# Modulations by streaming matmuls, made layer by layer between the first groups; loads reordered; the next layer's first scores in the last MLP step

## The chip, the cores and the metric

One core of a Trainium2 chip runs the whole program in one launch. The metric is the device time in microseconds, lower is better. [...] An engine that waits holds back everything behind the wait in its stream.

## The reference

Four transformer layers on x of [32, 128, 144] (32 sequences, 128 tokens, 144 channels), each conditioned by a row of `cond` [32, 144]:

```python
mod = silu(c) @ w_ada + b_ada                  # [32, 864]
sh1, sc1, g1, sh2, sc2, g2 = split(mod, 6)     # tanh on the gates in layer 2
x = x + g1 * attention(norm(x) * (1 + sc1) + sh1)        # 16 heads of 9 channels
x = x + g2 * mlp(norm(x) * (1 + sc2) + sh2)              # hidden 576
```

Layer 0's MLP is a mixture of four experts with the best two weighted by softmax. Layers 0, 1 and 3 use LayerNorm; layer 2 uses RMS norm, and norms q and k by head too. All in float32; the weights come in float32.

## The kernel before

The 32 sequences are eight groups of four; a group has 512 tokens. x stays in SBUF (`X`). Because 144 = 128 + 16 channels, every product over channels is two matmuls: one over the first 128 and one over the 16 others, held in split form with the bias rows (66 rows, in float32r). `split_chunk` on VectorE makes that form of the weights, from a staging tile (3 slots) that `load_chunk` on SyncE fills.

**The head.** SyncE first issues the loads of `si`, `sir` (the condition, 128 and 16 rows), `ident`, `masks`, the block mask and four gains (L294 to L301, one semaphore `q_c`), then layer 0's modulation weights, X of the first 8 sequences (576 KB), the q/k/v and projection weights, the other three layers' modulation weights and the rest of X in one DMA (L315). Then it waits for each layer's gates and stores them to a scratch (L316 to L319), issues three more chunks and `far_weights()` (23 DMAs: q/k/v and projection weights of layers 1 to 3, the expert weights of layer 0), and only then enters `attention(0)`. ScalarE makes silu after all of `q_c`. TensorE then makes the modulations of all four layers (`layer_mods`, L480): the weights are the stationary operand and the condition, 32 columns, the moving one, for shift and scale of the main 128 channels; the same for the 16 others repeated four times (that copy is made by VectorE's `replicate`); and the gates the other way round, with 144 columns. VectorE moves the results into `modm` and `modr` (`take_mods`), ScalarE the gates into `gsb`. The engines enter `attention(0)` when all four layers are done.

**Attention.** A group goes through statistics (`stats`, VectorE), the factor (`factor`, GpSimd), normalisation (`rows` on GpSimd or `normalise` on VectorE), the copy of the 16 channels (`copies`), transposes (`t_main`, `t_rem`), modulation (`mod_main` ScalarE, `mod_rem` VectorE), rounding (`round_rem`, `split_rem`), and the q/k matmuls (`q_and_k`). q and k are split in three bf16 parts (`part1` ScalarE, `rest1` VectorE, `parts23` GpSimd), written to a DRAM scratch (`write_parts`, 4 DMAs) and read back in another layout (`read_parts`, 12 DMAs) into one of three slots of `qk`. Groups are prepared two ahead: q and k of group n+2 are made while group n is attended to.

A group's attention is eight units U of two times four heads. For each, `scores_for_max` (TensorE, banks 0 and 1) and `head_max` (VectorE) give the maxima of the rows, `turn_max` and `max_out` turn them, `scores` makes the scores again, transposed and with the maxima taken off, ScalarE's exp follows, then `weigh`, `to_tokens`, `normed`. `scores_for_max` runs AHEAD = 5 units before `scores`. At the start of a layer `start_layer` (L645) makes these five units first, each waiting for the maxima of the one before, as both use banks 0 and 1.

In the first half of the program the slots of `qk` also hold the modulation weights, so that the first reads of `read_parts` wait for the end of the modulations. After each group SyncE issues the load of the gates for the next (`load_gates`), and in layer 0 two chunks. In layer 1 it issues the MLP weights of layers 1 to 3 in one go after the first group (`late_weights`, L340, 18 DMAs).

**The MLP.** For each group: five hidden tiles (`first`, two matmuls each), gelu on ScalarE, then `second` for each of the four sequences (five accumulating matmuls, each two passes); four experts one after another in layer 0. On VectorE follow the weighting (`experts`) and the gated product (`gated`), and GpSimd adds to X. Other work of the next layer's first groups is woven in by `after_tile` and `after_seq`.

Of the kernel before, what the change touches and what calls it, by code (L numbers as in the profile page):

```python
# [7 lines left out]
F32 = mybir.dt.float32  # L8
# [9 lines left out]
HID = 576  # L18
E = 4
# [68 lines left out]
BY_POOL = [k for l in range(L) for k in ([0, 1, 2, 3] if l == 0 else []) + [turned_at(l, g) for g in range(1, 7)]  # L88
           + [16 * l + 10, 16 * l + 11]]
BY_DVE = [k for l in range(L) for g in range(8) for k in prepared_mlp(l, g)]  # L90
# [11 lines left out]
def build(nc, io):  # L102
    ctx = ExitStack()
    with ctx:
# [77 lines left out]
        maskf = prob_f[0:TB, 0:2 * T].rearrange("p (a t) -> p a t", a=2)  # L182
# [4 lines left out]
        def turned_v(n):  # L187
# [5 lines left out]
        gsb = parts[0:B].rearrange("p m a t -> p (m a t)").bitcast(F32)[:, 0:L * 2 * C].rearrange("b (l n) -> b l n", l=L)  # L193
        qk_f = qk[:].rearrange("p a r h t -> p (a r h t)").bitcast(F32)
        ada = qk_f[:, 0:L * 6 * C].rearrange("p (l n) -> p l n", l=L)
        adar = qk_f[0:CR_CH + 1, L * 6 * C:2 * L * 6 * C].rearrange("p (l n) -> p l n", l=L)
        ada4 = qk_f[:, 2 * L * 6 * C:2 * L * 6 * C + 2 * 2 * 4 * 4 * CR_CH] \
            .rearrange("p (a k n) -> p a k n", a=4, k=4)
# [11 lines left out]
        q_c, q_x0, q_x1, q_w0 = sem("q_c"), sem("q_x0"), sem("q_x1"), sem("q_w0")  # L210
# [4 lines left out]
        q_gs, q_out = sem("q_gs"), sem("q_out")  # L215
# [18 lines left out]
        g_x, g_ew, g_ox, d_xn = sem("g_x"), sem("g_ew"), sem("g_ox"), sem("d_xn")  # L234

# [44 lines left out]
        def _(sp):  # L280
            def load_chunk(i):
# [6 lines left out]
                sp.dma_start(stage[0:4 * CR_CH, staged(i), 0:n], src.unsqueeze(0).to_broadcast([4, CR_CH, n])) \  # L288
                    .then_inc(done, 16)
                if bias is not None:  # L290
                    sp.dma_start(stage[4 * CR_CH:REM, staged(i), 0:n], bias.unsqueeze(0).to_broadcast([2, n])) \
                        .then_inc(done, 16)

            sp.dma_start(si[:], io.cT[0:CM]).then_inc(q_c, 16)  # L294
            sp.wait_ge(d_set, CR + 1)
            sp.dma_start(sir[0:CR_CH], io.cT[CM:C]).then_inc(q_c, 16)
            sp.dma_start(ident[:], io.ident).then_inc(q_c, 16)
            sp.dma_start(masks[:], io.masks).then_inc(q_c, 16)
            sp.dma_start(maskf, io.block_mask).then_inc(q_c, 16)
            for i, a in enumerate(io.gains):  # L300
                sp.dma_start(gains[:, i:i + 1], a.unsqueeze(0).to_broadcast([128, 1])).then_inc(q_c, 16)  # L301
            sp.dma_start(ada[:, 0, :], io.ada_w[0][0:CM, :]).then_inc(q_ada[0], 16)
            sp.dma_start(adar[0:CR_CH, 0, :], io.ada_w[0][CM:C, :]).then_inc(q_ada[0], 16)
            sp.dma_start(adar[CR_CH:CR_CH + 1, 0, :], io.ada_b[0].unsqueeze(0)).then_inc(q_ada[0], 16)
            xv = io.x.rearrange("b t c -> t b c")
            sp.dma_start(X[:, 0:2 * G, :], xv[:, 0:2 * G, :]).then_inc(q_x0, 16)
            sp.dma_start(wqkv[:, 0, :], io.qkv_w[0][0:CM, :]).then_inc(q_w0, 16)
            sp.dma_start(wproj[:, 0, :], io.proj_w[0][0:CM, :]).then_inc(q_w0, 16)
            for i in range(NEAR):
                load_chunk(i)  # L310
            for l in range(1, L):
# [3 lines left out]
            sp.dma_start(X[:, 2 * G:B, :], xv[:, 2 * G:B, :]).then_inc(q_x1, 16)  # L315
            for l in range(L):  # L316
                sp.wait_ge(a_gt, CR + l + 1)
                sp.dma_start(gate_scr[l].rearrange("w b c -> b w c"), gsb[:, l, :].rearrange("b (w c) -> b w c", w=2)) \
                    .then_inc(q_gs, 16)  # L319
            for i in range(NEAR, NST + NEAR):  # L320
                load_chunk(i)
# [10 lines left out]
            def far_weights():  # L332
                for l in range(1, L):
                    sp.dma_start(wqkv[:, l, :], io.qkv_w[l][0:CM, :]).then_inc(q_w1, 16)
                    sp.dma_start(wproj[:, l, :], io.proj_w[l][0:CM, :]).then_inc(q_w1, 16)
                sp.dma_start(wgate[:], io.gate_w[0:CM, :]).then_inc(q_w1, 16)
                for e in range(E):
                    load_mlp(L - 1 + e, q_w1)

            def late_weights():  # L340
                sp.wait_ge(s_y, CR + y_base[1])
                for i in range(EARLY, len(chunks)):
                    load_chunk(i)
                for l in range(1, L):
                    load_mlp(l - 1, q_w2)
# [31 lines left out]
            def read_parts(l, n):  # L377
                p, r = n % 2, n % 3
                if n < 3:
                    sp.wait_ge(d_mod, CR + L)  # L380
                    sp.wait_ge(s_ada, CR + L)
                else:
# [41 lines left out]
            def attention(l):  # L424
                n0, m0 = 8 * l, 16 * l
                if l == 0:
                    sp.wait_ge(q_gs, 16 * L)
                    load_gates(0)
                    for n in range(2):
                        write_parts(0, n)  # L430
# [1376 lines left out]
```

## Time and profile before

| | us |
|---|---|
| median of 3 runs | 1697.54 (1695.68 to 1697.6) |
| the profiled execution | 1692.07 |
| its span | 1690.3 |
| TensorE busy | 1512.2 (89%) |
| VectorE busy | 957.0 (57%) |
| ScalarE busy | 817.0 (48%) |
| GpSimd busy | 544.2 (32%) |
| TensorE's part of the chain that ended last | 62% |
| DMA's part of it | 14% |

Shares are of the span. The chain is followed back from the last instruction, at each step to what released it. Times in the rows below are from the span's start. A row such as `[7.51 <-POOL xr L1635]` says that the engine stood idle for 7.51 us before the instruction, until GpSimd's write of `xr` at line 1635 released it. The rows of `SPq` are SyncE's issuing of DMAs, not the transfers.

### The profile page before, as it was taken

To read this page: it belongs to the slowest core of one execution; us is meant where nothing else is said; L and a number is where in the kernel's file an instruction comes from. 1 tells how busy PE (TensorE), PEld (TensorE's weight loads), DVE (VectorE), ACT (ScalarE), POOL (GpSimd) and SP (SyncE) were. 2 spreads that over 40 slices of the span, in tenths; PEclk is the share of its full clock that TensorE was granted. 3 is DMA by queue.
4 is the path that set the end of the run, shared out by engine and by line. 5 is a ranking of instruction groups with operands and counts; after the bars stand their busy time and mean duration, and the time that the engine had idled before them with its cause. 6 is when DMAs were issued, how large, how long until landed. Compare 5 with 4: busy or idle time off the path is not lost.

```text
span 1690.3 us, 42551 instructions
## 1 busy us (share of the span) xinstructions
PE 1512.2 (89%) x16240; PEld 1116.7 (66%) x16240; DVE 957.0 (57%) x2662; ACT 817.0 (48%) x1687; POOL 544.2 (32%) x751
## 2 busy tenths in 40 slices
PE   6659998999999998879899968878799899998998
PEld 4436666777777776656667746656577666766777
DVE  2368886233343333768744778898535566665442
ACT  0246676233333322657655436666554455555543
POOL 0535553111131210444432323424334324432321
PEclk9979999999999998989999979999899989998999
DMA  4445551000021020554501243443223767676021
GB/s 118 137 117 133 133 129 37 8 7 8 8 50 29 29 50 1 120 137 115 112 17 35 56 93 79 103 104 86 65 48 39 110 108 112 100 121 113 16 60 47
DMA packets 209275, 126.30 MB, mean 75 GB/s; under 512 B 143873, under 2 KB 192608, under 8 KB 203890
## 3 DMA queue, kind: packets, MB, share of 16 engines
q1 hardware_dynamic: 190386, 121.21, 32.8%
q10 hardware_dynamic: 18688, 2.36, 1.1%
q8 instruction: 132, 2.16, 0.6%
q14 instruction: 69, 0.57, 0.1%
HBM read 89.56 MB, written 33.18 MB: 73 GB/s over the span
## 4 chain that ended last, share of the span: by engine, by line
PE 62%; DMA 14%; DVE 9%; SPq 8%; issue 5%; POOL 1%; ACT 1%; DVEq 0%; POOLq 0%; ACTq 0%
PE bank L850 15%; PE bank L832 13%; DMA qk<-qk_scr 7%; PE bank L613 4%; PE bank L578 4%; PE bank L833 4%; DVE negm L1329 4%; SPq L403 3%; PE bank L641 3%; SPq L374 2%; PE bank L621 2%; PE bank L597 2%; PE bank L534 2%; DMA v_scr<-wfc 2%; PE bank L601 2%
## 5 line engine op out<-in xcount | busy, mean ns | idle before, releaser
L1061 ACT ACTIVATE prob<-bank 128x512 f32<-128x512 f32 x512 | 278.0, 595 | 245.9 <-PE bank L601 245.1
L1329 DVE TENSOR_REDUCE negm<-bank 128x4 bf16<-128x512 f32 x512 | 334.0, 682 | 104.2 <-PE bank L578 100.2
L1180 ACT ACTIVATE hid<-bank 128x512 f32<-128x512 f32 x280 | 166.7, 596 | 351.9 <-PE bank L833 351.2
L850 PEld LDWEIGHTS bank<-wfc,hid 128*128 128x128 f32 (+1 forms) x2240 | 285.8, 192 | 11.6 <-issue 9.1
L850 PE MATMUL bank<-wfc,hid 128*128 128x144 f32 (+1 forms) x2240 | 290.8, 287 | 0.2 <-DVE gx L1359 0.2
L832 PE MATMUL bank<-hT,wfc 128*128 128x512 f32 x560 | 290.4, 599 | 0.0
L1655 POOL TENSOR_TENSOR X<-X,gx 128x288 f32<-128x288 f32 x128 | 100.7, 800 | 429.7 <-DVE gx L1359 427.0
L833 PE MATMUL bank<-hr,rfc 66*128 66x512 f32 x280 | 224.7, 802 | 0.0
L578 PE MATMUL bank<-qk 54*128 54x128 bf16 (+1 forms) x2048 | 125.1, 245 | 94.0 <-DVE negm L1329 49.9
L613 PE MATMUL bank<-prob,V 128*32 128x128 f32 x4096 | 173.8, 290 | 2.4 <-ACT OT L1067 2.4
L597 PE MATMUL bank<-qk 54*128 54x128 bf16 (+1 forms) x2048 | 172.0, 239 | 4.1 <-ACT prob L1061 4.1
L601 PE MATMUL bank<-mT,pick 64*128 64x128 bf16 x2048 | 169.0, 229 | 0.0
L578 PEld LDWEIGHTS bank<-qk 54*128 54x128 bf16 (+1 forms) x2048 | 71.2, 103 | 141.0 <-DVE negm L1329 67.6
L1640 POOL CAST parts<-res 96x512 bf16<-96x512 f32 x96 | 59.2, 617 | 267.1 <-DVE res L1279 266.0
L1478 DVE SCALAR_TENSOR_TENSOR On<-bank,cw,On 128x144 f32<-128x144 f32 x96 | 30.8, 363 | 199.1 <-PE bank L850 199.1
L832 PEld LDWEIGHTS bank<-hT,wfc 128*128 128x128 f32 x560 | 102.0, 191 | 60.2 <-ACT hid L1180 33.2
L1266 DVE TENSOR_SCALAR hmod<-bank,modr 64x128 f32<-64x128 f32 x256 | 86.9, 396 | 90.7 <-PE bank L511 90.4
L613 PEld LDWEIGHTS bank<-prob,V 128*32 128x32 f32 x4096 | 100.9, 113 | 42.7 <-issue 27.0
L1008 ACT ACTIVATE hT<-bank,modm 128x128 f32<-128x128 f32 x256 | 98.5, 452 | 42.1 <-PE bank L504 42.1
L597 PEld LDWEIGHTS bank<-qk 54*128 54x128 bf16 (+1 forms) x2048 | 109.6, 102 | 9.2 <-ACT prob L1061 6.4
L1642 POOL TENSOR_TENSOR parts<-res,parts 96x512 bf16<-96x512 f32 x96 | 111.3, 1160 | 7.8
L1067 ACT ACTIVATE OT<-bank 128x256 f32<-128x256 f32 x256 | 99.2, 388 | 23.3 <-PE bank L613 11.4
(151 smaller groups left out, 2326.8 us busy)
## 6 DMA issues: line engine op xcount, KB each, us to landing
qk<-qk_scr SPq DMA_DIRECT2D x336, 72.0 KB
gbuf<-gate_scr SPq DMA_DIRECT2D x64, 288.0 KB, 4.0
qk_scr<-parts SPq DMA_DIRECT2D x48, 288.0 KB, 2.5
qk<-qk_scr SPq DMA_DIRECT2D x48, 216.0 KB
qk<-tok_scr SPq DMA_DIRECT2D x112, 72.0 KB
qk_scr<-parts SPq DMA_DIRECT2D x48, 144.0 KB, 2.4
qk<-qk_scr SPq DMA_DIRECT2D x48, 144.0 KB
tok_scr<-parts SPq DMA_DIRECT2D x48, 96.0 KB, 4.7
```

Source lines behind the costliest of these rows:

```text
L578: mm = pe.matmul(bank[s][:, T * i:T * i + T], operand(l, 0, n, U, s, i), operand(l, 1, n, U, s, i), start=True, stop=True)
L597: pe.matmul(bank[2 + s][:, at], operand(l, 1, n, U, s, i), operand(l, 0, n, U, s, i), start=True, stop=False)
L601: mm = pe.matmul(bank[2 + s][:, at], pick[half, 4 * (u % 2) + i, :], mT[half, u // 2, :], start=False, stop=True)
L613: mm = pe.matmul(bank[4][32 * i:32 * i + 32, T * s:T * s + T], V[:, n % 3, u // 2, VS * h:VS * h + 32], prob[:, 2 * (U % 2) + s, T * i:T * ...
L832: pe.matmul(bank[2 + i % 2][:], wfc1_t[:, at:at + 128], hT[:, h, :], start=True, stop=False)
L833: pe.matmul(bank[2 + i % 2][:], rfc1_t[:, at:at + 128], hr[:, h, :], start=False, stop=True) \
L850: mm = pe.matmul(bank[4 + q][:, C * (b % 2):C * (b % 2) + C], hid[0:rows, t, T * b:T * b + T], wfc2[0:rows, k, t, :], start=(t == 0), stop ...
L1061: act.activation(prob[:, 2 * (U % 2) + s, :], bank[2 + s][:], ACT.Exp, scale=scale).then_inc(a_exp, 1)
L1180: act.activation(hid[0:rows, t, :], bank[2 + i % 2][0:rows, :], func).then_inc(a_gelu, 1)
L1329: dve.tensor_reduce(negm[:, b, s, 4 * (u % 2):4 * (u % 2) + 4], bank[s][:].rearrange("q (h k) -> q h k", k=T), AX.X, ALU.max, negate=True) ...
L1642: pool.tensor_tensor(parts[:, m, 2, :], res[:, i % 2, :], parts[:, m, 1, :], ALU.subtract).then_inc(g_p3, 1)
L1655: pool.tensor_tensor(x, x, gx[:, q, :, :], ALU.add).then_inc(g_x, 1)
```

## The change

The modulations of a layer are now four matmuls: the condition is stationary (32 columns) and the weights stream, 432 columns for each half of a layer. Attention's and the MLP's half go to partitions 0 to 31 and 32 to 63 of bank 7. VectorE copies shift and scale out (`mods_out`), TensorE transposes them back to channels on partitions (`turn_mods`, four transposes into bank 4), VectorE adds the one and stores (`take_mods`), ScalarE takes the gates (`gates`). The four layers are placed between the steps of the first three groups. The modulation weights lie in other slots of `qk`, so that group 0's reads need not wait for them.

```diff
+            def layer_mods(l):
+                pe.wait_ge(q_ada[l], 48)
+                if l:
+                    pe.wait_ge(d_ms, CR + l)
+                    pe.wait_ge(a_gt, CR + l)
+                for w in range(2):
+                    out, cols = bank[7][B * w:B * w + B, 0:3 * C], slice(3 * C * w, 3 * C * w + 3 * C)
+                    pe.matmul(out, si[:], ada[:, l, cols], start=True, stop=False)
+                    mm = pe.matmul(out, sir[:], adar[:, l, cols], start=False, stop=True)
                 mm.then_inc(s_ada, 1)
+            def turn_mods(l):
+                pe.wait_ge(d_ms, CR + l + 1)
+                if l:
+                    pe.wait_ge(d_mod, CR + l)
+                for s in range(2):
+                    pe.transpose(bank[4][:, 2 * B * s:2 * B * s + 2 * B], mods_m[:, s, :], ident[0:2 * B, 0:2 * B])
...
```

TensorE's order in `attention(0)`, before `start_layer`:

```diff
+                    layer_mods(0)
+                    turn_mods(0)
                     t_rem(0, 5)
                     t_main(0, 6)
+                    for m in range(3):
+                        q_and_k(l, 0, m, m)
+                    layer_mods(1)
                     t_rem(1, 5)
                     t_main(1, 6)
                     values(l, 0, 0, 3)
                     values(l, 0, 1, 4)
                     for m in range(3):
+                        pe.wait_ge(d_r1, CR + m + 1)
                         q_and_k(l, 1, m, m)
+                    turn_mods(1)
+                    layer_mods(2)
                     t_rem(2, 5)
                     t_main(2, 6)
+                    turn_mods(2)
+                    layer_mods(3)
+                    turn_mods(3)
+                    pe.wait_ge(d_mod, CR + 4)
                     values(l, 1, 0, 3)
                     values(l, 1, 1, 4)
...
+                    pe.wait_ge(a_gt, CR + L)
+                    pe.wait_ge(d_set, CR + 3)
```

ScalarE has `gates(l)` at 0 before `mod_main(0)`, 1 before `mod_main(1)`, 2 before `mod_main(2)`, 3 after `round_rem(2)`. VectorE, which now normalises groups 0 to 2 in GpSimd's place:

```diff
+                    dve.wait_ge(q_x[0], 16)
                     stats(0)
+                    mods_out(0)
+                    split_chunk(0)
+                    normalise(0)
+                    take_mods(0)
                     stats(1)
                     mod_rem(0, 5)
                     split_rem(0)
+                    normalise(1)
                     for m in range(3):
                         rest1(0, m, m)
+                    mods_out(1)
                     mod_rem(1, 5)
                     split_rem(1)
+                    stats(2)
+                    normalise(2)
                     for m in range(3):
                         rest1(1, m, m)
+                    take_mods(1)
+                    mods_out(2)
                     mod_rem(2, 5)
                     split_rem(2)
+                    take_mods(2)
+                    mods_out(3)
+                    set_up()
+                    take_mods(3)
+                    split_chunk(1)
+                    dve.wait_ge(q_x3, 16)
                     stats(3)
```

(`head_max` of the first units follows; `set_up` holds the copies and memsets that stood before everything.) SyncE starts with the modulation weights; the small loads, the silu and the second chunk go to ScalarE's queue:

```diff
+            load_ada(0)
+            sp.dma_start(X[:, 0:G, :], xv[:, 0:G, :]).then_inc(q_x[0], 16)
+            load_chunk(0)
+            sp.dma_start(wqkv[:, 0, :], io.qkv_w[0][0:CM, :]).then_inc(q_w0, 16)
+            sp.dma_start(X[:, G:2 * G, :], xv[:, G:2 * G, :]).then_inc(q_x[1], 16)
+            load_ada(1)
+            sp.dma_start(X[:, 2 * G:3 * G, :], xv[:, 2 * G:3 * G, :]).then_inc(q_x[2], 16)
+            load_ada(2)
+            load_ada(3)
...
+                    write_parts(0, 0)
+                    read_parts(0, 0)
+                    for i in range(L):
+                        save_gates(i)
+                    write_parts(0, 1)
+                    read_parts(0, 1)
+                    sp.wait_ge(q_gs[0], 16)
                     load_gates(0)
+                    sp.dma_start(X[:, 3 * G:B, :], xv[:, 3 * G:B, :]).then_inc(q_x3, 16)
+                    for i in range(NEAR, NST + NEAR):
+                        load_chunk(i)
...
                     load_gates(m0 + g + 1)
+                    if l == 0 and g < 5:
+                        far_weights(g)
                     if l == 0 and 1 <= g <= 4:
                         for i in range(3 + 2 * g, 5 + 2 * g):
                             load_chunk(i)
-                    if l == 1 and g == 0:
-                        late_weights()
+                    if l == 1:
+                        late_weights(g)
```

`save_gates(l)` waits for the gates of layer l and stores them. `read_parts(0, 1)` waits for all modulations. `far_weights(g)` issues one expert's four DMAs and, for g of 1 to 3, two of layer g's weights; `late_weights(g)` the six chunk DMAs at g = 0 and four DMAs of one layer's MLP at g = 1, 3 and 5.

The first five units of layers 1 and 3 move into the last MLP step of the layer before (in layer 0 into the last expert's `second`):

```diff
+                    if l in (0, 2) and g == 7:
+                        if b == 0 and l == 0:
+                            pe.wait_ge(d_top, CR + 2 * 8)
+                        if b == 0 and l == 2:
+                            pe.wait_ge(q_mask, 16 * 12)
+                        scores_for_max(l + 1, UNITS * N + b)
+                        if b == 3:
+                            scores_for_max(l + 1, UNITS * N + 4)
...
+                            if g == 7 and e == E - 1:
+                                first_maxima()
                             for q in range(2):
                                 experts(g, e, q)
                         dve.wait_ge(d_y, CR + Y_OF[0] * (g + 1))
+                    if l == 2 and g == 7:
+                        first_maxima()
                     for q in range(2):
```

`first_maxima` is the ten `head_max` of those units. `start_layer` keeps the scores only for layers 0 and 2, with the turns of the maxima where they were.

## Rows read from the trace of the kernel before

**Rows 1.** Busy time by stretches: engines, granted clock, DMA share, GB/s.
```profile
13.60:52.70 39.10, 39.09 (x160) 27.95 (x160) 5.16 (x28) 1.20 (x3) 0.00 (x0) 1.00 0.34 94
...
10.00:27.50 17.50, 13.89 (x55) 10.69 (x56) 6.08 (x26) 0.75 (x3) 0.00 (x0) 1.00 0.95 272
...
85.00:95.00 10.00, 0.00 (x1) 0.03 (x2) 2.71 (x9) 2.03 (x4) 6.15 (x9) 0.53 0.68 166
```
**Rows 2.** Groups by form, 13.6 to 52.8: busy us, mean ns, idle before.
```profile
L495 PE MATMUL bank<-qk,si 128*32 128x144 f32 x16 | 5.5, 448 | 0.0
...
L1197 ACT ACTIVATE parts<-bank 32x288 f32<-32x288 f32 x4 | 1.6, 399 | 40.6 <-PE bank L496 40.6
```
**Rows 3.** Instructions in order of time: start, us, instruction, idle before it.
```profile
10.66 0.23 ACT L1193 ACTIVATE si<-si 128x32 f32<-128x32 f32 x1 [7.57 <-DMA gains<-in_L_cond_kg]
...
53.42 0.94 DVE L1238 BATCH_NORM_STATS2 stat<-X 128x6 f32<-128x144 f32 x4
...
60.25 1.03 PE L511 MATMUL bank<-ident,xr 128*64 128x128 f32 x4 [7.51 <-POOL xr L1635]
...
65.28 1.99 PE L534 MATMUL bank<-hT,wqkv 128*96 128x512 f32 x2 [3.15 <-DVE hr L1272]
...
69.06 1.02 PE L534 MATMUL bank<-hT,wqkv 128*96 128x512 f32 x2
...
95.62 1.29 DVE L1329 TENSOR_REDUCE negm<-bank 128x4 bf16<-128x512 f32 x2 [7.71 <-PE bank L578]
```
**Rows 4.** The chain that ended last, in order of time: start, us.
```profile
84.59 10.27 DMA qk<-qk_scr
...
301.01 4.92 PE bank L850 x40
```
**Rows 5.** Layer 1, SyncE's issuing, and one TensorE row.
```profile
699.61 0.34 SPq L350 DMA_DIRECT2D gbuf<-gate_scr  x1
...
718.04 1.94 SPq L371 DMA_DIRECT2D qk_scr<-parts  x4
...
830.46 19.09 SPq L350 DMA_DIRECT2D gbuf<-gate_scr  x2
...
742.09 0.61 PE L578 MATMUL bank<-qk 54*128 54x128 bf16 x8 [7.54 <-DMA qk<-qk_scr]
```
**Rows 6.** DMA issues: count, KB each, median us from issue to landing.
```profile
qk_scr<-parts SPq DMA_DIRECT2D x48, 288.0 KB, 2.5
...
X<-in_x SPq DMA_DIRECT2D x1, 576.0 KB, 6.2
```
**Rows 7.** The gate loads (line 350), 0 to 300 us.
```profile
L350 SPq DMA_DIRECT2D gbuf<-gate_scr x9: 319/342/346, 67.3 to 286.0; - x9
...
DMA to landing us min/median/max: 3.2/10.7/12.0
```
**Rows 8.** Layer 0, SyncE's issuing, and one TensorE row.
```profile
56.27 0.36 SPq L334 DMA_DIRECT2D wqkv<-in_L_cond_W_qkv  x1
...
129.95 0.34 SPq L350 DMA_DIRECT2D gbuf<-gate_scr  x1
...
136.85 7.71 SPq L371 DMA_DIRECT2D qk_scr<-parts  x4
...
250.68 35.69 SPq L350 DMA_DIRECT2D gbuf<-gate_scr  x3
...
140.50 0.40 PE L578 MATMUL bank<-qk 54*128 54x128 bf16 x8 [0.53 <-DMA qk<-qk_scr]
```
**Rows 9.** The two borders between layers, in order of time.
```profile
657.55 5.08 PE L850 MATMUL bank<-wfc,hid 128*128 128x144 f32 x40
...
672.11 0.29 PE L597 MATMUL bank<-qk 54*128 54x128 bf16 x2
...
1340.87 7.11 PE L850 MATMUL bank<-wfc,hid 128*128 128x144 f32 x40
...
1346.52 1.15 DVE L1257 TENSOR_SCALAR xn<-X,mv,rstd 128x144 f32<-128x144 f32 x4 [1.48 <-POOL rstd L1601]
...
1356.77 0.30 PE L597 MATMUL bank<-qk 62*128 62x128 bf16 x2
```

More of the change, by code:

```diff
@@ L208, in build @@
         gate_scr = nc.dram_tensor("gate_scr", [L, 2, B, C], F32, kind="Internal").ap()
-        q_c, q_x0, q_x1, q_w0 = sem("q_c"), sem("q_x0"), sem("q_x1"), sem("q_w0")
+        q_si, q_id, q_c, q_w0 = sem("q_si"), sem("q_id"), sem("q_c"), sem("q_w0")
+        q_wp = sem("q_wp")
+        q_x, q_x3 = [sem(f"q_x{i}") for i in range(3)], sem("q_x3")
         q_ada = [sem(f"q_ada{l}") for l in range(L)]
@@ L214, in build @@
         q_late, q_w2 = [sem(f"q_late{i}") for i in range(L - 1)], sem("q_w2")
-        q_gs, q_out = sem("q_gs"), sem("q_out")
+        q_gs, q_out = [sem(f"q_gs{l}") for l in range(L)], sem("q_out")
         q_w = sem("q_w")
@@ L330, in load_mlp, with far_weights, late_weights @@
                 sp.dma_start(wfc2[TAIL:TAIL + 1, at, KT - 1, :], b2.unsqueeze(0)).then_inc(done, 16)
[L332 to L345, printed above, removed]
+            def far_weights(g):
+                if g < E:
+                    load_mlp(L - 1 + g, q_w1)
+                if 0 < g < L:
+                    sp.dma_start(wqkv[:, g, :], io.qkv_w[g][0:CM, :]).then_inc(q_w1, 16)
+                    sp.dma_start(wproj[:, g, :], io.proj_w[g][0:CM, :]).then_inc(q_w1, 16)
+                if g == 0:
+                    sp.dma_start(wgate[:], io.gate_w[0:CM, :]).then_inc(q_w1, 16)
+            def late_weights(g):
+                if g == 0:
+                    sp.wait_ge(s_y, CR + y_base[1])
+                    for i in range(EARLY, len(chunks)):
+                        load_chunk(i)
+                if g % 2 and g // 2 < L - 1:
+                    load_mlp(g // 2, q_w2)
             def load_gates(i1):
@@ L466, in mlp @@
                             .then_inc(q_out, 16)
-            far_weights()
             for l in range(L):
@@ L987, in mlp @@
                         q_and_k_by_token(N + 2, b, 7 - b % 2)
-            pe.wait_ge(q_c, 16 * 9)
             pe.wait_ge(a_si, CR + 2)
-            for l in range(L):
-                layer_mods(l)
+            pe.wait_ge(q_id, 16 * 2)
             for l in range(L):
@@ L1005, in mod_main @@
                 act.wait_ge(s_ht, CR + NTH[k] + 1)
+                if k == 0:
+                    act.wait_ge(d_mod, CR + 1)
                 for b in seqs:
@@ L1081, in attention @@
                 if l == 0:
+                    gates(0)
                     mod_main(0, 6)
@@ L1085, in attention @@
                         part1(0, m, m)
+                    gates(1)
                     mod_main(1, 6)
@@ L1385, in attention @@
                 for U in range(64 * l, 64 * l + AHEAD):
-                    for s in range(2):
-                        head_max(l, U, s)
+                    if l in (0, 2):
+                        for s in range(2):
+                            head_max(l, U, s)
                     if U % 2 == 0 and U > 64 * l:
@@ L1479, in experts, with first_maxima @@
                     ins.then_inc(d_y, 1)
+                def first_maxima():
+                    for U in range(UNITS * N, UNITS * N + AHEAD):
+                        for s in range(2):
+                            head_max(l + 1, U, s)
                 for g in range(8):
@@ L1659, in attention @@
                 if l == 0:
-                    prepare(0)
-                    prepare(1)
+                    for k in range(2):
+                        factor(k)
+                        copies(k)
                     pool.wait_ge(g_xr, CR + 2)
```

215 lines of the change are left out of this document (93 added, 122 removed).

## The prediction

> **What bounds the kernel now.** I read the table by stretches first [rows 1]. From 13.6 to 52.7 us TensorE is the only engine at work (39.09 of 39.10 us; ScalarE 1.20, GpSimd 0), and from 85 to 95 us it does nothing. Over the span it is busy 89%, so the rest is dense, and the head of the program is the target. The form table of that stretch [rows 2] says what fills it: small f32 matmuls that make the modulations, 160 passes for four layers [rows 1], while ScalarE stands idle before them for 40.6 us. The instructions in time [rows 3] give the head's frame: silu held until 10.66 by the last of nine small loads, LayerNorm of group 0 from 53.42, its first transposes at 60.25, first q/k matmul at 65.28, first pair of maxima at 95.62. The chain of waits [rows 4] fills the gap before the last: the twelve reads of the q/k scratch end 10.3 us after the last was issued (84.59). My anchor for the head is the first pair of maxima, 95.6.
>
> The queue's own list in layer 1 [rows 5] shows a second hole. Between the reads of group 10 (its gate load follows them, 699.61) and the writes of group 11 (718.04), SyncE issues 18 weight DMAs, and TensorE then stands 7.54 us at 742.09. The five intervals between gate loads are 130.8 us there (699.61 to 830.46) and 120.7 in layer 0 (129.95 to 250.68) [rows 5, 8]: 10.1 lost, 7.54 of it standing.
>
> The sum is made against the profiled execution: 1690.3 span, 1692.07 in all. The median of the timed runs, 1697.54, is 5.5 higher; I add that at the end.
>
> **The modulations.** A layer was 20 matmuls in two passes each, 9.8 us (39.1 over 4). It becomes 4 matmuls of 432 columns, so 8 passes, and 4 small transposes. A 144-column pass takes 0.34 here [rows 2] and 4.92/40 = 0.123 in the MLP [rows 4]: the head runs at the lower of the two levels, 1.2 GHz, although its granted clock is printed as 1.00 [rows 1]. The 512-column f32 passes take 1.0 each at 65.28 and 0.5 at 69.06 [rows 3]. Scaled by columns, one of 432 costs 0.84 or 0.43: 6.7 or 3.4 a layer, the two bounds. Since the array now streams, I take 5.3 for the first layer (slow, then fast) and 3.3 for each of the other three.
>
> **The head, step by step.** Silu waits for two small loads only, issued by about 3.5. The first modulation weights head SyncE's queue, issued by 2.0; an X load of 576 KB takes 6.2 us to land and a store of parts 2.5 [rows 6]. So the matmuls start between 4.5 and 8.2; I take 7.0, with the end at 12.3. Two copies out of the bank, four transposes (the like take 1.03, rows 3), VectorE's split, its four normalisations (1.15, rows 9) and GpSimd's copy put group 0's first transposes at 15.7 instead of 60.25. From there to the first reads the order is the old one, so they land at 94.9 - 44.5 = 50.4.
>
> Group 0's maxima don't start then, because of the new orders:
> - TensorE: q/k of group 0 20.7 to 25.6; layer 1's modulations to 28.9; group 1's transposes and values to 31.3; q/k of group 1 (behind modulation, rounding and split) 33.5 to 38.5; layer 2 to 43.1; group 2's transposes and the turns to 47.4; layer 3 to 50.7.
> - VectorE copies it at 51.4, ScalarE makes the fourth gates at 51.8. SyncE has waited for them in `save_gates(3)`, ahead of group 1's writes. Those go out 52.5 to 54.3 and land at 56.9 (2.5, rows 6); the reads are issued to 64.3; the gate load and the last X load follow, at 65.1.
> - VectorE's program has `wait_ge(q_x3)` and `stats(3)` ahead of the first `head_max`, so all maxima are queued behind an X load that stands behind group 1's twelve reads.
>
> A gate load issued straight behind reads lands 10.7 us later in the median, 3.2 at best [rows 7]. The X load brings 20 x 128 x 144 x 4 = 1.47 MB more, 5.4 us at the 272 GB/s of 10 to 27.5 us; reads leave engines idle (share 0.68 in 85 to 95) [rows 1], so I take 1 us off. It lands at 80.2; statistics (0.94, rows 3, and by estimate a third of it for the aggregation) make it 81.5. Gain 14.1 of 44.5. The set-up copies (estimate 3 us of VectorE) lie beside SyncE's chain and cost nothing; without that cover, 3. Bounds of the gain: 4 (slow array throughout) to 23 (X lands by itself).
>
> The Trainium skill bears on this (DMA: Bandwidth & Descriptors, "Queues, rings and completion order"): completion is not first-in first-out per issuing engine, since one DMA is split over up to 16 rings. The gate loads (10.7 against 3.2) show no overtaking in the median. By the page alone the X load could be early, and the sum that of the third rival below.
>
> **Far weights into attention of layer 0.** 23 DMAs stood ahead of everything, from 56.27 [rows 8], under TensorE's modulations and transposes. Now 5 follow group 0's gate load, and 6 those of groups 1 to 3, beside four chunk loads. The reads are just in time: TensorE stood 0.53 for them at 140.50. SyncE is free from 130.3 to 136.85, and the writes go out over 7.7 us, to 144.6 [rows 8]. Ten DMAs of about 0.5 take 5 us, their 1.2 MB 4 us behind the reads' landing. Cost per group between 0 and 10.1 (what 18 cost in layer 1), for three groups; I take 2 in all, near the low end, because the last write is needed only 14 us after the gate load, and in layer 1 the queue came free after 18.4.
>
> **Late weights of layer 1 spread.** Six chunk DMAs remain behind group 10's gate load (3.2 us), so the writes go at the usual 6.9 after it (129.95 to 136.85). The 7.54 stall goes, and the slow stretch after it (eight scores in 0.61 there, rows 5, against 0.40, rows 8). Four weight DMAs follow in each of three later groups, 2 us of SyncE. Between 5 and 10.1; I take 8.5.
>
> **First scores in the last MLP step.** Five sets of score matmuls and five pairs of maxima move at each of two borders, none goes. End of layer 0: four blocks of the second matmul run from 657.55, 1.27 each (5.08/4) [rows 9]. With 0.40 of scores behind each and 1.29 for a pair of maxima [rows 3], the pairs start at 659.2, 661.0, 662.7, 664.6 and 666.4 and end at 667.7. Behind them on VectorE wait two experts and two gated products (2.1) and two copies of maxima around a turn (0.7), all by estimate: first `scores` at 670.5 instead of 672.11. Gain 1.6. End of layer 2: the maxima stand behind `normalise`, which ends at 1347.7. TensorE, in order, has done two of the four blocks (7.11/4 = 1.78 each) when the second scores wait for the first maxima at 1348.9. Then come 0.6 of scores, 1.8 of block, twice, and two more rounds of 2.0; the maxima end at 1357.6, gated products, copies and turn 1.6: `scores` at 1359.2 instead of 1356.77 [rows 9]. Loss 2.4. Bounds: +4 to -2 for the first border, +2 to -5 for the second.
>
> **Sum.** 14.1 - 2 + 8.5 + 1.6 - 2.4 = 19.8: profile about 1672.3, median 1677.7.
>
> **The rivals.**
> - The array stays slow in the modulations. For: it did so for 39 us at a busy share of one [rows 1, 2]. Against: those passes were mostly of 32 columns, and the 512-column ones sped up within four us. Three layers at +3.4 and the first at +1.4, 11.6, of which 1.6 hides beside other work: 1687.7. Chance 0.20.
> - Nothing holds the maxima, and the first group's lead is kept: 29 us more, 1648.7. Against: VectorE's program order. Chance 0.04.
> - The X load ends on its own, 6.5 after its issue (6.2 for 576 KB) and so 8.6 earlier: 1669.1. For: DMA engines idle during reads. Against: the gate loads. Chance 0.17.
> - Slower: in layer 0 the weights between reads and writes clog the queue as the 18 did in layer 1, 10.1 at each of groups 1 to 3, +30.3 for the 2 in the sum: 1706.0. It decides when SyncE comes free later than 14 us after the gate load. For: TensorE waits for reads already. Against: ten DMAs, not eighteen. Chance 0.07.
> - The forecast: 0.50. The last 0.02 is for what none of these covers.
>
> **Range and chances.** The forecast's own range is 1671 to 1684. With the slow array and the early load in it, 1664 to 1691 leaves out the kept lead and the clogged queue. 0.2% (3.4 us) is about what a measurement of this kernel can tell from no change. Faster by more: 0.90; within: 0.03 (slow array with some clogging); slower: 0.07.
>
> **What would show it.** First maxima near 81, VectorE idle until the X load lands, though group 0's reads landed near 50. Four blocks of 3.3 to 5.3 us for the modulations, the last ending near 51. In layer 1 the five intervals between gate loads take 121 to 123, without a stall of 7; in layer 0 they grow by at most 2. In layer 3 the first `scores` comes later after the last `normalise` than the 9.1 us of before. Wrong would be: maxima at 55 to 60 or at 90; stalls of over 2 us for reads in several groups of layer 0.

## The result

| | before | after |
|---|---|---|
| median, us | 1697.54 (1691.54 to 1706.29, 7 runs) | 1684.29 (1679.72 to 1689.29, 7 runs) |
| ratio | 1 | 0.993, 95% interval 0.9901 to 0.9959 |
| profiled execution, its span | 1692.07, 1690.3 | 1686.7, 1684.9 |
| granted clock over the span | 0.949 | 0.942 |

Faster, as forecast, but by 13.3 us and not 19.8: 0.3 us outside the forecast's own range (1671 to 1684) and inside the wide one (1664 to 1691). Executions of one kernel lie 5 to 9 us to either side of their median, so I compare stages, each between two instructions that both kernels have:

| stage, us | before | after | forecast of the difference | measured |
|---|---|---|---|---|
| start to first maxima of group 0 | 95.6 | 80.2 | -14.1 | -15.4 |
| first `scores` of layer 0 to its first `first` | 188.6 | 201.1 | +2 | +12.5 |
| MLP of layer 0, to layer 1's first `scores` | 379.8 | 376.5 | -1.6 | -3.3 |
| attention of layer 1 | 200.2 | 192.7 | -8.5 | -7.5 |
| MLP of layer 1, attention of layer 2 | 363.4 | 363.9 | 0 | +0.5 |
| MLP of layer 2, to layer 3's first `scores` | 121.1 | 124.5 | +2.4 | +3.4 |
| attention of layer 3 | 237.9 | 242.4 | 0 | +4.5 |

The stages add up to the 5.4 us between the two profiled executions, not to 13.3: the one of before was 5.5 us under its median, the one of after 2.4 us above. One term is far off: attention of layer 0. In the rows PE is TensorE, DVE VectorE, ACT ScalarE, POOL GpSimd and SP SyncE. Lines have moved in the changed kernel: `scores_for_max` is L589, `scores` L608, `head_max` L1374, the gate load L349, the writes of parts L370.

### The profile page after: what moved, and what is told of

Read it like the earlier page. It is cut to its first block and busy times, and to the rows that moved or that the text cites. A ratio compares the mean times of both kernels' runs of the same rounds, so it can differ in the third digit from the quotient of the medians.

```text
span 1684.9 us, 42331 instructions
## 1 busy us (share of the span) xinstructions
PE 1498.2 (89%) x16128; PEld 1098.2 (65%) x16128; DVE 957.5 (57%) x2666; ACT 816.5 (48%) x1687; POOL 533.8 (32%) x739
## 5 line engine op out<-in xcount | busy, mean ns | idle before, releaser
L1374 DVE TENSOR_REDUCE negm<-bank 128x4 bf16<-128x512 f32 x512 | 333.7, 681 | 105.5 <-PE bank L589 101.8
L871 PE MATMUL bank<-wfc,hid 128*128 128x144 f32 (+1 forms) x2240 | 294.4, 289 | 0.2 <-DVE gx L1404 0.2
L589 PE MATMUL bank<-qk 54*128 54x128 bf16 (+1 forms) x2048 | 124.8, 244 | 100.3 <-DVE negm L1374 68.0
L608 PE MATMUL bank<-qk 54*128 54x128 bf16 (+1 forms) x2048 | 172.3, 239 | 8.4 <-ACT prob L1090 5.9
L589 PEld LDWEIGHTS bank<-qk 54*128 54x128 bf16 (+1 forms) x2048 | 71.2, 103 | 146.8 <-DVE negm L1374 84.6
L608 PEld LDWEIGHTS bank<-qk 54*128 54x128 bf16 (+1 forms) x2048 | 110.3, 103 | 11.0 <-ACT prob L1090 8.3
L1096 ACT ACTIVATE OT<-bank 128x256 f32<-128x256 f32 x256 | 99.1, 387 | 25.0 <-PE bank L624 13.2
```

The lines of the kernel that those rows point to most:

```text
L589: mm = pe.matmul(bank[s][:, T * i:T * i + T], operand(l, 0, n, U, s, i), operand(l, 1, n, U, s, i), start=True, stop=True)
L608: pe.matmul(bank[2 + s][:, at], operand(l, 1, n, U, s, i), operand(l, 0, n, U, s, i), start=True, stop=False)
L871: mm = pe.matmul(bank[4 + q][:, C * (b % 2):C * (b % 2) + C], hid[0:rows, t, T * b:T * b + T], wfc2[0:rows, k, t, :], start=(t == 0), stop ...
L1374: dve.tensor_reduce(negm[:, b, s, 4 * (u % 2):4 * (u % 2) + 4], bank[s][:].rearrange("q (h k) -> q h k", k=T), AX.X, ALU.max, negate=True) ...
```

## The profile after

**The head**, TensorE in order of time (start, us, instruction, idle before it), beside [rows 3]:

```profile
9.01 1.62 PE L496 MATMUL bank<-qk,si 128*32 128x432 f32 x2 [9.01 <-DMA masks<-in_masks]
...
18.58 1.06 PE L522 MATMUL bank<-ident,xr 128*64 128x128 f32 x4 [1.82 <-POOL xr L1698]
...
23.46 1.99 PE L545 MATMUL bank<-hT,wqkv 128*96 128x512 f32 x2 [2.97 <-DVE hr L1317]
...
28.34 0.91 PE L496 MATMUL bank<-qk,si 128*32 128x432 f32 x2
...
46.78 0.91 PE L497 MATMUL bank<-qk,sir 17*32 17x432 f32 x2
```

Layer 0's four modulation matmuls take 6.4 us, 1.62 for two passes of 432 columns; the other three layers' take 3.4 each, at 0.91. So the array is at the lower level (1.2 GHz) when it begins and at the upper one when it comes back at 28.34, in work that streams 512 columns in between. (The profile prints a granted clock of 1.00 from 9 to 16 us all the same, as for the head of before.) The rows above end at 47.7 (forecast 50.7). Then VectorE and TensorE, in the same columns:

```profile
79.03 0.94 DVE L1283 BATCH_NORM_STATS2 stat<-X 128x6 f32<-128x144 f32 x4 [26.46 <-DMA X<-in_x]
79.89 0.36 DVE L1288 BATCH_NORM_AGGREGATE mv<-stat 128x2 f32<-128x6 f32 x4
80.16 1.25 DVE L1374 TENSOR_REDUCE negm<-bank 128x4 bf16<-128x512 f32 x2
...
81.48 0.61 PE L589 MATMUL bank<-qk 54*128 54x128 bf16 x8 [25.19 <-DVE negm L1374]
```

VectorE stands 26.46 us for the last X load, and TensorE behind it. SyncE's own list says when that load went out, and what followed:

```profile
49.23 2.04 SPq L370 DMA_DIRECT2D qk_scr<-parts  x4
...
60.91 0.34 SPq L349 DMA_DIRECT2D gbuf<-gate_scr  x1
61.29 0.44 SPq L434 DMA_DIRECT2D X<-in_x  x1
61.77 13.16 SPq L294 DMA_DIRECT2D hid<-in_L_cond_w_gate  x1
```

**Layer 0.** The stretch of five gate-load intervals, and 15 us of it (columns as in [rows 1]); before, the five took 120.7 by the starts in [rows 8]:

```profile
120.00:125.00 5.00, 5.00 (x58) 2.90 (x57) 4.68 (x8) 4.34 (x9) 2.46 (x4) 1.00 1.01 150
125.00:130.00 5.00, 1.10 (x14) 0.67 (x14) 0.98 (x3) 0.59 (x1) 1.07 (x1) 0.89 0.65 142
130.00:135.00 5.00, 5.00 (x59) 4.05 (x55) 2.34 (x4) 1.98 (x5) 2.53 (x3) 0.50 0.44 136
115.54:249.88 134.34, 119.10 (x1941) 86.20 (x1939) 108.16 (x255) 84.83 (x180) 63.07 (x80) 0.95 0.66 145
```

The same stretch of the kernel before:

```profile
129.95:250.68 120.73, 112.53 (x1921) 81.14 (x1921) 106.98 (x252) 83.57 (x178) 62.01 (x78) 1.00 0.53 131
```

Two lessons are in these rows. The DMA engines are busy 0.66 of the time, not 0.53, and wholly so from 120 to 125, while group 2's reads are still under way and the first parts of group 3 go out. And the 13.6 us are two nearly equal halves: TensorE is idle 15.2 instead of 8.2 (+7.0), and busy 119.1 instead of 112.5 (+6.6) for the same work, as the granted clock behind some of the pauses is about half (0.50 from 130 to 135). TensorE's two longest pauses there, and the landing of the writes (24 of them, minimum, median, maximum; [rows 6] has 2.5 as the median before):

```profile
129.45 0.39 PE L589 MATMUL bank<-qk 54*128 54x128 bf16 x3 [3.90 <-DMA qk<-qk_scr]
...
179.58 0.21 PE L608 MATMUL bank<-qk 54*128 54x128 bf16 x1 [2.50 <-issue]
```
```profile
L370 SPq DMA_DIRECT2D qk_scr<-parts x24: 304/333/1550, 99.7 to 239.7; - x24
...
DMA to landing us min/median/max: 2.2/3.9/6.3
```

What came late for the 3.90 were group 2's reads. Their last issue, the first weight load behind them, group 3's four writes and GpSimd's work on the last part, in the kernel after:

```profile
115.18 0.32 SPq L402 DMA_DIRECT2D qk<-qk_scr  x1
...
115.92 0.43 SPq L323 DMA_DIRECT2D wfc<-in_L_cond_w  x1
...
122.44 11.30 SPq L370 DMA_DIRECT2D qk_scr<-parts  x4
...
131.51 0.61 POOL L1703 CAST parts<-res 96x512 bf16<-96x512 f32 x1 [5.45 <-DVE res L1324]
```

And the last of the same reads in the kernel before:

```profile
129.59 0.32 SPq L403 DMA_DIRECT2D qk<-qk_scr  x1
```

From the end of that issue to TensorE's first use of the reads are 10.6 us before (129.91 to 140.50, [rows 8]) and 14.0 after (115.50 to 129.45), with five weight loads issued right behind the reads. The four writes take 11.3 us to go instead of 7.7 because of the pause and not the other way round: the last part is made only after TensorE has gone on. Nor do the slower landings hold the next reads: they are issued from 136.01, 2.3 us after the writes' end, as before (146.81, 2.3 after 144.56).

**Layer 1** answers to [rows 5]: SyncE, then the five intervals.

```profile
692.62 0.34 SPq L349 DMA_DIRECT2D gbuf<-gate_scr  x1
...
699.07 7.91 SPq L370 DMA_DIRECT2D qk_scr<-parts  x4
```
```profile
692.62:816.09 123.47, 112.99 (x1921) 81.26 (x1919) 102.01 (x242) 83.74 (x179) 61.20 (x79) 1.00 0.59 136
```

The writes follow the gate load by 6.45 us instead of 18.4, the intervals take 123.5 instead of 130.8, and no stall over 3.3 us is left.

**The borders** answer to [rows 9]. The first row is the first block of the last `second` of layer 0; then the first scores of layer 1, the last `normalise` of layer 2 and the first maxima behind it, and the first scores of layer 3:

```profile
653.11 1.15 PE L871 MATMUL bank<-wfc,hid 128*128 128x144 f32 x8
...
665.83 0.29 PE L608 MATMUL bank<-qk 54*128 54x128 bf16 x2
...
1334.06 1.15 DVE L1302 TENSOR_SCALAR xn<-X,mv,rstd 128x144 f32<-128x144 f32 x4 [1.48 <-POOL rstd L1664]
1335.12 1.28 DVE L1374 TENSOR_REDUCE negm<-bank 128x4 bf16<-128x512 f32 x2
...
1336.46 0.64 PE L589 MATMUL bank<-qk 62*128 62x128 bf16 x8 [3.71 <-DVE negm L1374]
...
1346.98 0.30 PE L608 MATMUL bank<-qk 62*128 62x128 bf16 x2
```

From first block to first scores 12.7 us, before 14.6: gain 1.8. From the end of the last `normalise` (1335.2) to the first scores 11.8, before 9.1: loss 2.7, of which TensorE stands 3.71 in one piece for the queued maxima.

## The experiments

The ratios are to the kernel before, run beside each on the same chip. The stages of all of them (us; "five" are the five gate-load intervals):

| | first maxima | attention 0 | five of layer 0 | five of layer 1 | MLP 2 | median | ratio |
|---|---|---|---|---|---|---|---|
| before | 95.6 | 188.6 | 120.7 | 130.8 | 121.1 | | 1 |
| after | 80.2 | 201.1 | 134.3 | 123.5 | 124.5 | 1684.29 | 0.993 |
| e1 | 81.5 | 189.0 | 120.9 | 121.6 | 123.1 | 1676.59 | 0.9877 |
| e2 | 58.2 | 196.6 | 128.6 | 127.1 | 125.1 | 1664.32 | 0.9811 |
| e3 | 57.0 | 195.9 | 122.1 | 129.4 | 125.4 | 1659.80 | 0.9799 |
| e4 | 81.9 | 202.0 | 131.3 | 125.2 | 121.7 | 1680.29 | 0.9904 |
| e5 | 95.9 | 188.8 | 120.4 | 128.1 | 122.7 | 1689.13 | 0.9965 |
| e6 | 95.4 | 200.8 | 128.8 | 127.3 | 120.9 | 1700.73 | 1.0053 |
| e7 | 55.7 | 194.2 | 125.2 | 124.1 | 121.2 | 1649.39 | 0.9746 |
| e8 | 79.4 | 196.1 | 127.5 | 122.6 | 126.9 | 1675.55 | 0.9919 |
| e9 (e7 again) | 55.9 | 188.6 | 120.6 | 124.0 | 121.0 | 1639.24, one run | |
| e10 | 81.0 | 204.1 | 134.0 | 125.2 | 125.0 | 1691.01 | 0.9960 |

**e1: the far weights out of layer 0's attention.** The changed kernel with them ahead of group 0's attention.

```diff
                     for i in range(1, L):
                         sp.wait_ge(q_gs[i], 16)
+                    for i in range(5):
+                        far_weights(i)
...
-                    if l == 0 and g < 5:
-                        far_weights(g)
```

> Base: the changed kernel; the 23 DMAs of the far weights are issued in one go before group 0's attention (SyncE has nothing to issue from 78 to 99 us) instead of behind the reads of groups 0 to 3. Theory A (far weights between a group's reads and the next writes lengthen layer 0's attention; from its first scores to the MLP's first matmul it took 201.1 us against 188.6 before): that stretch returns to 187 to 191, the stall of 3.9 us for reads at 129 goes, total 10 to 13 us under the changed kernel's, 0.983 to 0.988 of before. Rival B (the stretch is longer because of the earlier start or the late last X load, whatever SyncE issues): it stays at 198 to 202 and the total within 3 us of the changed kernel's.

Ratio 0.9877 (0.9843 to 0.991). Attention of layer 0 is back at 189.0, clock 1.00, write landings at a median of 2.5. From 96 to 270 us TensorE has no wait for reads; the changed kernel has three, 6.2 us in all. That is theory A; the time is 9 us under the changed kernel's by the ratios, a little short of its 10 to 13:

```profile
118.74:239.59 120.85, 113.20 (x1945) 81.64 (x1935) 107.78 (x255) 84.30 (x180) 63.34 (x80) 1.00 0.55 133
```

**e2: the X load early**, behind the modulation weights in SyncE's head.

```diff
             load_ada(3)
+            sp.dma_start(X[:, 3 * G:B, :], xv[:, 3 * G:B, :]).then_inc(q_x3, 16)
...
                     load_gates(0)
-                    sp.dma_start(X[:, 3 * G:B, :], xv[:, 3 * G:B, :]).then_inc(q_x3, 16)
```

> Base: the changed kernel; the last X load (20 sequences) is issued right behind the fourth layer's modulation weights instead of behind group 1's reads. Theory A (the first maxima wait only for that load): first pair of maxima at 55.5 to 57.5 us instead of 80.2, VectorE's 26.5 us of idle time gone, total about 23 us under the changed kernel's, 0.976 to 0.981 of before. Rival B (next in line are group 1's reads, or the queue fills and holds back group 0's writes): maxima start early but TensorE stands for group 1's reads, and less than 15 us is left of the 24.

Ratio 0.9811 (0.9778 to 0.9844), some 20 us under the changed kernel. VectorE, first maxima:

```profile
58.21 1.29 DVE L1374 TENSOR_REDUCE negm<-bank 128x4 bf16<-128x512 f32 x2 [2.60 <-PE bank L589]
```

The 26.46 us of waiting are gone, and it is now the score matmuls that release the maxima, 0.7 us later than theory A's range. So the place of one load in a queue decided 22 us of the head.

**e3: both edits.**

```diff
+            sp.dma_start(X[:, 3 * G:B, :], xv[:, 3 * G:B, :]).then_inc(q_x3, 16)
...
+                    for i in range(5):
+                        far_weights(i)
```

> Base: the changed kernel with both moves: last X load behind the modulation weights, far weights in one go before group 0's attention. Theory A (the two losses are separate): gains add, first maxima near 56, first scores to the MLP's first matmul 187 to 192 us, total 33 to 36 us under the changed kernel's, 0.969 to 0.974 of before. Rival B (the far weights now stand behind group 1's reads, before group 2's writes, and cost there what they cost spread): less than 27 us.

Ratio 0.9799 (0.976 to 0.9838): by the ratios 22 us under the changed kernel, which is rival B's range. Against e2 it is 4.5 us less by the medians and 2 by the ratios, whose intervals overlap, and not the 9 that e1 gave. With the head 22 us shorter, the 23 far weights behind group 1's reads run into group 2's writes; SyncE and TensorE:

```profile
66.66 0.36 SPq L324 DMA_DIRECT2D wfc<-in_L_cond_w  x1
...
72.18 1.79 SPq L325 DMA_DIRECT2D wfc<-in_L_cond_w  x1
...
85.22 2.81 SPq L371 DMA_DIRECT2D qk_scr<-parts  x4
...
108.14 0.61 PE L589 MATMUL bank<-qk 54*128 54x128 bf16 x8 [5.44 <-DMA qk<-qk_scr]
```

Here it is the queue that holds: SyncE issues weights up to the writes, which start at 85.22 and not at 78.47 as in e2, and all four go within 2.8 us where e2's take 7.1: their parts had been waiting.

**e4: layer 3's first units back at the start of the layer**, border 2 to 3 alone undone.

```diff
-                    if l in (0, 2) and g == 7:
+                    if l in (0,) and g == 7:
...
-                    if l == 2 and g == 7:
-                        first_maxima()
```

> Base: the changed kernel; the first five units of layer 3 are made at the start of layer 3 again, those of layer 1 stay in the last expert's step. Theory A (the move costs at that border because the maxima stand behind the normalisation and TensorE in order behind them): from the MLP's first matmul in layer 2 to the first scores of layer 3 121 us instead of 124.5, total 3 to 4 us less. Theory A2 (the late gated product and the late stretch also lengthen layer 3's attention, 242.4 against 237.9 us): 7 to 8 us less. Rival B (executions of one kernel differ by more than that, and the border is neutral): within 2 us.

Ratio 0.9904 (0.9865 to 0.9942); MLP of layer 2 121.7; the six kernels with the border as changed have 123.1 to 126.9 there (mean 125.0), the four as it was before 120.9 to 122.7 (mean 121.6). The size, 3.4, is near the 2.7 of the rows. By the ratios the whole is 4.4 us less, but the intervals overlap, so the time can't tell theory A from the other two. Attention of layer 3, on which theory A2 rests, is 239.3 here against 242.4.

**e5: the kernel before with the late weights spread, alone.**

```diff
-                    if l == 1 and g == 0:
-                        late_weights()
+                    if l == 1:
+                        late_weights(g)
```

> The kernel before, with one thing changed: layer 1's loads of the next MLP weights are spread over groups 0, 1, 3 and 5 instead of being issued together at group 0. Theory A (the spread takes the queue's pile-up out of layer 1's gate loads and the 7.5 us stall of TensorE at the second group): 7 to 10 us less than the kernel before, ratio about 0.995, layer 1's attention near 192 instead of 200. Theory B (each part of the loads only stalls a later group instead): within 2 us, attention of layer 1 198 to 201.

Ratio 0.9965 (0.9938 to 0.9991): 5.9 us, with an interval of 1.5 to 10.5 that reaches into both theories' ranges. Attention of layer 1 is 198.6, which is theory B's range, not the 192 of theory A. The stall of 7.54 [rows 5] is 2.44 (TensorE):

```profile
737.70 0.40 PE L579 MATMUL bank<-qk 54*128 54x128 bf16 x8 [2.44 <-DMA qk<-qk_scr]
```

The one profile shows only 2.8 off the five intervals, with a pause of 1.87 in it that no release explains. Over the ten profiles with the spread the five intervals are 121.6 to 129.4, mean 125.1; the two without it have 130.8 and 127.3. So it is worth 4 to 6 us by these two estimates, no more exactly than that, and the 7.3 between the two profiles of before and after probably overstate it.

**e6: the kernel before with the far weights in attention, alone.**

```diff
-            far_weights()
...
+                    if l == 0 and g < 5:
+                        far_weights(g)
```

> The kernel before, with one thing changed: the far weights are no longer loaded ahead of group 0's attention but behind the gate loads of layer 0's groups 0 to 4. Theory A (this alone is what lengthens layer 0's attention after the change): layer 0's attention grows by 10 to 13 us, the first maxima stay near 95.6, ratio 1.006 to 1.008. Theory B (the growth needs the earlier start of the changed kernel, for which the reads then come late): layer 0's attention within 3 us of 188.6, ratio 0.998 to 1.002.

Ratio 1.0053 (1.0027 to 1.0078), attention of layer 0 200.8, first maxima where they were (95.4). This is theory A and the clean price of that edit: 9 us as time (4.6 to 13.2), 12.2 in the profile, and nothing earned by it in the head.

**e8: only the wide rows spread.** The changed kernel, with the experts' second matrices and biases issued ahead of group 0's attention.

```diff
+                    for i in range(E):
+                        load_mlp(L - 1 + i, q_w1, (2,))
...
-                    load_mlp(L - 1 + g, q_w1)
+                    load_mlp(L - 1 + g, q_w1, (1,))
```

> The changed kernel, with the loads of the experts' second matrices and biases (rows of 576 bytes, three DMAs for each expert) issued ahead of group 0's attention; only the wide rows (first matrices, qkv, projection, gate) stay behind the gate loads of groups 0 to 4. Theory A (the many short rows are what delays the groups' writes and reads): layer 0's attention 189 to 192 instead of 201.1. Theory B (bytes or DMAs of any kind between the reads and the next write do it): 195 to 199.

Ratio 0.9919 (0.989 to 0.9948), attention 196.1: with twelve DMAs taken out, 5 of the 12.5 us are gone. Theory B's range; there is a pause of 1.66 without a releaser in this profile too, so that the share of the short rows is not settled.

**e10: the same DMAs from another queue.** The far weights issued by ScalarE.

```diff
-                    if l == 0 and g < 5:
-                        far_weights(g)
...
+                        if l == 0 and g < 5 and u >= 5:
...
+                            for dst, src in far_weights(g)[2 * (u - 5):2 * (u - 4)]:
+                                act.dma_start(dst, src).then_inc(q_w1, 16)
```

> The changed kernel, with the far weights issued by ScalarE's queue instead of SyncE's, the same DMAs in the same stretch (two behind each of units 5, 6 and 7 of layer 0's groups 0 to 4). Theory A (what delays the groups' writes and reads is that the weights stand ahead of them on SyncE's own queue): layer 0's attention falls from 201.1 to 189 to 192 us, plus up to 3 for ScalarE's issuing. Theory B (it is the data on the shared DMA engines, whatever queue brings it): 197 to 203.

Ratio 0.996 (0.9939 to 0.9981), not under the changed kernel's 0.993. Attention is 204.1 in the profile, which is that of the slowest of ten executions (1697.65, median 1691.01): nothing is won. SyncE's queue no longer holds the weights, and the groups' reads are as late (TensorE; then the five intervals, with the DMA engines' share):

```profile
130.80 0.40 PE L587 MATMUL bank<-qk 54*128 54x128 bf16 x8 [3.52 <-DMA qk<-qk_scr]
...
211.70 0.61 PE L587 MATMUL bank<-qk 54*128 54x128 bf16 x8 [4.17 <-DMA qk<-qk_scr]
```
```profile
117.36:251.31 133.95, 116.54 (x1923) 84.24 (x1921) 107.27 (x252) 84.16 (x179) 62.51 (x79) 0.96 0.60 141
```

Group 2's reads are all issued by 117.32 here, with nothing but the gate load behind them on SyncE before the next writes, and TensorE gets them 13.5 us later, as in the changed kernel (14.0) and not as before (10.6). So it is the data on the DMA engines that delays the reads, not SyncE's order. What ScalarE's own issuing adds was not measured apart. The Trainium skill says of this (DMA: Bandwidth & Descriptors, "Issuing engines are not separate DMA queues"): DMAs started by different engines run on the same 16 DMA engines and interleave. The traces agree, with 13.5 and 14.0.

**e7: the version that the others point to.** X early; the far weights right behind it in the head, but the second matrices of two experts, whose place holds the gates, behind group 1's reads; and `first_maxima()` ahead of layer 2's last `normalise`.

```diff
+            sp.dma_start(X[:, 3 * G:B, :], xv[:, 3 * G:B, :]).then_inc(q_x3, 16)
...
+            for i in range(5):
+                far_weights(i)
...
+                    if l == 2 and g == 7:
+                        first_maxima()
```

> The changed kernel, with three things changed: the load of X for groups 3 and up is issued behind the modulation weights in the head; the far weights are issued right behind it, except the second matrices of the first two experts, which follow group 1's reads; at the border of layers 2 and 3 the next layer's first maxima are issued ahead of the last normalise. Theory A (the three costs add): first maxima near 57, layer 0's attention 188 to 190, MLP of layer 2 118 to 121, some 33 to 40 us under the changed kernel, ratio to the kernel before 0.970 to 0.975. Theory B (the early loads hold up group 0's write and reads on the shared DMA engines): first maxima at 62 or later, or layer 0's attention 195, ratio 0.978 or more.

Ratio 0.9746 (0.9726 to 0.9767), 44 us under the kernel before and, by the ratios, some 31 under the changed one, 2 short of what was expected. First maxima 55.7, MLP of layer 2 121.2. Over their ranges were MLP of layer 2, by 0.2, and attention of layer 0, at 194.2, with no wait for reads over 1 us. It has two pauses without a releaser, and the clock behind the longer (TensorE, then windows):

```profile
196.35 0.23 PE L614 MATMUL bank<-qk 54*128 54x128 bf16 x2 [1.80 <-issue]
```
```profile
194.00:196.00 2.00, 0.55 (x14) 0.39 (x13) 2.00 (x6) 0.59 (x1) 0.11 (x1) 1.00 0.56 135
196.00:198.00 2.00, 1.65 (x28) 1.05 (x27) 0.35 (x1) 0.92 (x2) 1.65 (x2) 0.62 0.59 124
198.00:200.00 2.00, 2.00 (x11) 1.42 (x7) 0.74 (x1) 1.65 (x4) 0.00 (x0) 0.52 0.77 205
```

**e9: e7 once more**, unchanged, for these pauses.

> The kernel of e7 once more, for a second look at two pauses of TensorE that no semaphore explains (1.48 and 1.80 us, at 126.42 and 196.35) and that cost layer 0's attention some 4 us with the fall of the clock behind the second. Theory A (they come and go from execution to execution): at least one is gone or elsewhere, and layer 0's attention is 189 to 192. Theory B (they belong to the order of this kernel): both again within 1 us of the same places and attention 193 to 195. First maxima at 55 to 57 by either.

Both are gone, attention is 188.6, and the execution took 1639.24 (one execution, on another chip; the kernel before took 1690.73 beside it):

```profile
91.37:212.01 120.64, 112.90 (x1935) 81.44 (x1929) 107.59 (x254) 84.40 (x180) 62.91 (x79) 1.00 0.53 132
```

So they are not fixed to this kernel's order; what makes them I have not found.

## Why the prediction was right, and where not

- **The head** held as a mechanism and nearly as a size: the X load behind group 1's reads held VectorE's `stats(3)`, and all maxima queued behind it. (Group 1's reads are 18 DMAs, not twelve.) The modulations began at 9.01, past their latest bound of 8.2, and the first transposes of group 0 at 18.58 instead of 15.7; the shorter steps behind them made that good. Issued 3.8 earlier than forecast (61.29 against 65.1), it took 17.7 us to land instead of 15.1. e2 shows the cause by taking it away.
- **The modulations**: 6.4 + 3 x 3.4 against 5.3 + 3 x 3.3. The rival of the slow array fell: 0.91 for two passes from 28.34 on. The rivals of an X load that ends early by itself and of a lead that is kept fell too. No run has the streaming form without the new order, so its own share of the gain stays open.
- **Far weights into attention of layer 0** is the step that failed, "I take 2 in all, near the low end": 12.5 in the profile, 9 as a time in e6. I asked when SyncE would be free to issue the writes. That was the wrong resource: the first write went out at 122.44, 6.9 behind the gate load as before [rows 8]. What came late were the reads that stood ahead of the weights: the last of group 2's reached TensorE 14.0 us after its issue instead of 10.6, and TensorE stood 3.90 for it. The row that warned stood in the sum: reads already just in time, a stall of 0.53 at 140.50 [rows 8]. With no slack, more data on the DMA engines at that moment becomes a pause of TensorE, and a pause can cost again as slow clock (+7.0 idle, +6.6 busy). The rival of a clogged queue put 10.1 on each of three groups; the truth was less than half of it, by another mechanism (e10). One of the changed kernel's pauses, 2.50 without a releaser, may be none of the edit's; with the slow clock behind it (0.52 and 0.63 from 180 to 184) it is some 4 of the 13.6 us, by estimate. But e4, which has the same layer 0, spent 202.0 on it with five waits for reads of 1.1 to 2.5 each, one pause of 1.39 without a releaser and hardly any fall of the clock:

```profile
118.52:249.84 131.32, 115.27 (x1949) 83.22 (x1945) 108.45 (x255) 84.76 (x180) 63.32 (x80) 0.99 0.67 147
```

  There the idle time grew by 7.9 and the busy time by 2.7: how much the clock adds varies with how the waits fall.
- **Late weights spread**: mechanism right, the stall of 7.54 gone and the writes 6.5 behind the gate load. Forecast 8.5; 7.3 in the profiles, 5.9 (1.5 to 10.5) as a time (e5).
- **The borders**: gains of +1.8 against +1.6 and -2.7 against -2.4, both from the rows; no run undid the first border alone. Calling the second a loss was right, and its cure (`first_maxima` ahead of `normalise`) brought MLP 2 to 121.2 and 121.0, the time of before; e7 changed it together with the loads.
- **Attention of layer 3**, +4.5, is in no term. The six profiles with the second border as changed have 237.6 to 247.0 there (mean 241.4), the four with it as before 237.9 to 239.3 (mean 238.6), e7 and e9 with the cure 239.5 and 237.9. So a part may belong to that border, as theory A2 of e4 says, and a part may be variation; it stays open.

The other errors nearly cancel, by luck and not by exact terms: with that edit alone undone the kernel takes 1676.59 (e1), where the sum without its 2 gives 1675.7.

## What to carry to other kernels

When loads are spread into a stretch whose transfers arrive just in time, price them by the busy share of the DMA engines at that moment too, and not only by when the issuing queue is free: here transfers issued ahead of them came late. Put them where nothing waits for the engines. Then ask for every load in the head who is queued behind it: here one load issued 50 us earlier gave 20 us, more than the whole change. A pause of TensorE in dense work can cost nearly twice its length, if the clock falls behind it: behind e7's 1.80 us the two windows shown lose about 1.7 us to it, by estimate.

## What the runs showed that I had not expected

- SyncE's issue of the small DMA behind the X load took 13.16 us (61.77, changed kernel), and 7.14 in e7, where a weight load stood behind the same load in the head; in e2, with the X load elsewhere, the small one took 0.62. Issuing is not free when a long load is ahead.
- After the pause of 3.90 us the granted clock is 0.50 from 130 to 135, after that of 1.80 (e7) 0.62 and 0.52 in two windows of 2 us, though TensorE is busy again; it had been 1.00 before. After the stall of 7.54 in the kernel before it was 0.53 from 742 to 748. It isn't so each time: after e4's wait of 2.48 for reads, which ended at 131.06, it stayed at 1.00.
- TensorE pauses of 0.8 to 2.5 us with no releaser appear in seven of the twelve profiles, all but two of them in layer 0's attention; neither of e7's came in a second execution of it. Their cause stays open.
